# Moving two products with V and one softmax division inside a transformer block on one core

## The reference, cut to what matters

```
x = x + attn_block(layernorm(x))       # inside: attention over a window of 15 neighbours, 16 heads of 16, then an MLP 256->1024->256
z = layernorm(x)
main = gelu(z @ W1m + b1m) @ W2m + b2m # 256 -> 1024 -> 256
logits = mean(z, over the tokens) @ w_gate + b_gate      # the two best of 8 experts, weights gate_w
expert_out = sum over the two of gate_w * (gelu(z @ W1e + b1e) @ W2e + b2e)
out = x + a * main + (1 - a) * expert_out
```

## Time and profile before

| what | value |
|---|---|
| median of 3 runs | 2020.44 us (2018.67 to 2022.75) |
| profiled execution: its time, its span | 2019.08 us, 2017.4 us |
| PE busy | 1983.6 us, 98% of the span |
| DVE, ACT, POOL busy | 73%, 56%, 46% of the span |
| mean granted TensorE clock | 0.996 |

### The profile page before, as it was taken

How to read it: one execution, slowest core, us unless ns; L and a number is a source line. 1 busy time by engine, 2 the same in 40 slices (tenths; PEclk the granted TensorE clock), 3 DMA queues, 4 the chain that set the end, 5 groups by cost and what they waited for, 6 DMA issues and landing times.

```text
span 2017.4 us, 37536 instructions
## 1 busy us (share of the span) xinstructions
PE 1983.6 (98%) x13456; PEld 1817.1 (90%) x13456; DVE 1470.9 (73%) x2466; ACT 1134.0 (56%) x1797; POOL 928.3 (46%) x909
## 2 busy tenths in 40 slices
PE   7889999999999999999999999999999999999999
PEld 6789999999999999999999999999999999999998
DVE  7577786877868678686877868678686786868743
ACT  4455565655556565565555556555564655655554
POOL 5435255362543635345362552625436353453635
PEclk9999999999999999999999999999999999999999
DMA  3121121211102121121211202111021211212111
GB/s 106 48 63 43 49 57 33 74 53 53 53 22 79 48 66 51 32 65 42 74 52 44 55 30 74 53 53 53 30 70 48 69 48 38 63 38 74 43 57 54
DMA packets 188848, 108.79 MB, mean 54 GB/s; under 512 B 65436, under 2 KB 187640, under 8 KB 188664
## 3 DMA queue, kind: packets, MB, share of 16 engines
q1 hardware_dynamic: 188088, 105.62, 18.4%
q10 hardware_dynamic: 576, 0.79, 0.1%
HBM read 85.52 MB, written 8.39 MB: 47 GB/s over the span
## 4 chain that ended last, share of the span: by engine, by line
PE 92%; DVE 4%; issue 1%; ACT 1%; POOL 0%; SPq 0%; DMA 0%; ACTq 0%; POOLq 0%; DVEq 0%
PE psB L233 50%; PE psA L233 26%; PE psA L1061 6%; PE psA L1088 5%; PE psA L1073 3%; PE psA L982 2%; DVE pr L621 1%; DVE smax L617 1%; DVE acc L559 1%; DVE qm L586 0%; DVE hr_lo L543 0%; POOL wf_lo L424 0%; PE psA L1105 0%; ACT hr_hi L845 0%; PE psB L1111 0%
## 5 line engine op out<-in xcount | busy, mean ns | idle before, releaser
L543 DVE TENSOR_TENSOR hr_lo<-hf,hr_hi 128x512 fp32r<-128x512 f32 x512 | 488.5, 954 | 436.0 <-ACT hr_hi L845 435.4
L845 ACT ACTIVATE hr_hi<-hf 128x512 fp32r<-128x512 f32 x512 | 323.9, 633 | 269.7 <-PE psB L233 182.5
L435 POOL TENSOR_TENSOR wx_lo<-raw,wx_hi 128x512 fp32r<-128x512 f32 x256 | 395.9, 1546 | 21.4
L433 POOL TENSOR_SCALAR wx_hi<-raw 128x512 fp32r<-128x512 f32 x256 | 188.6, 737 | 358.0 <-PE psB L233 344.0
L841 ACT ACTIVATE hf<-psB,b1x 128x512 f32<-128x512 f32 x256 | 175.0, 684 | 201.7 <-PE psB L233 200.7
L233 PE MATMUL psB<-wx_hi,hr_hi 128*128 128x256 f32 x1024 | 287.5, 281 | 0.2
L233 PE MATMUL psB<-wx_hi,hr_lo 128*128 128x256 f32 x1024 | 286.4, 280 | 0.0
L233 PE MATMUL psB<-wx_lo,hr_hi 128*128 128x256 f32 x1024 | 285.7, 279 | 0.0
L449 POOL TENSOR_SCALAR kb<-kT 64x384 f32<-64x384 f32 x128 | 81.7, 639 | 358.9 <-ACT kT L861 351.0
L233 PE MATMUL psB<-z_hi,wx_hi 128*128 128x512 f32 x512 | 210.9, 412 | 0.0
L233 PE MATMUL psB<-z_hi,wx_lo 128*128 128x512 f32 x512 | 202.5, 396 | 0.0
(11 more groups left out here) (149 smaller groups left out, 5132.4 us busy)
## 6 DMA issues: line engine op xcount, KB each, us to landing
raw<-in_L_ffn_W1e SPq DMA_DIRECT2D x256, 128.0 KB, 2.2
raw<-in_L_ffn_W2e SPq DMA_DIRECT2D x256, 128.0 KB, 2.1
out_x<-acc SPq DMA_DIRECT2D x32, 256.0 KB, 2.2
xin<-in_L_attn_x SPq DMA_DIRECT2D x15, 512.0 KB, 3.8
vb<-vs SPq DMA_DIRECT2D x64, 96.0 KB
vb<-vs SPq DMA_DIRECT2D x64, 80.0 KB
tm<-in_L_ffn_b2e SPq DMA_DIRECT2D x32, 128.0 KB, 3.0
raw<-in_L_attn_fc_w SPq DMA_DIRECT2D x8, 256.0 KB, 3.6
```

Source lines behind the costliest of these rows:

```text
L433: g.tensor_scalar(wx[0][:, s, :], raw[:, s, :], 1.0, 0.0, ALU.mult, ALU.add).then_inc(w_hi.sem, 1)
L435: g.tensor_tensor(wx[1][:, s, :], raw[:, s, :], wx[0][:, s, :].bitcast(f32), ALU.subtract).then_inc(w_lo.sem, 1)
L543: v.tensor_tensor(hr[1][:, c % 2, :], hf[:, c % 3, :], hr[0][:, c % 2, :].bitcast(f32), ALU.subtract).then_inc(h_lo.sem, 1)
L845: a.activation(hr[0][:, c % 2, :], hf[:, c % 3, :], ACT.Copy).then_inc(h_hi.sem, 1)
```

## The change

Three moves, with no instruction added or removed. On TensorE `attend(0)` goes from slot 6 to the end of slot 5, right behind `scores(2)`, and `attend(1)` from slot 8 to the end of slot 7, right behind `scores(3)`. On VectorE the block with `gather` is put behind the block with `normalise` in every slot; only in slot 9 do both blocks have something to do, so that `normalise(2)` now stands in front of `gather` of f0 to f7.

```
@@ VectorE
                 for q in range(NQ + 2):
-                    if q >= 2 and there(ORDER[q - 2][0], t) and ORDER[q - 2][0] == "f" and ORDER[q - 2][1] % KH == KH - 1:
-                        gather(t, ORDER[q - 2][1])
                     if t < ROWS:
                         if q == 3:
                             normalise(t, 0)
...
                         elif q == 15:
                             norm2_apply(t, 1)
+                    if q >= 2 and there(ORDER[q - 2][0], t) and ORDER[q - 2][0] == "f" and ORDER[q - 2][1] % KH == KH - 1:
+                        gather(t, ORDER[q - 2][1])
                     if q < NQ and there(ORDER[q][0], t):
                         h_low(t, *ORDER[q], q)
@@ TensorE
                     elif q == 5:
                         scores(t, 2)
+                        attend(t, 0)
                     elif q == 6:
-                        attend(t, 0)
                         turn(t, 1)
                     elif q == 7:
                         scores(t, 3)
-                    elif q == 8:
                         attend(t, 1)
```

## The result

The changed kernel takes 2078.53 us (median of 4 runs, 2077.54 to 2080.74), against 2019.89 before in the same session. The ratio is 1.0291, with a 95% interval of 1.0275 to 1.0306: slower by 58.6 us. The prediction was 2074, with a range of 2048 to 2094.

The account below looks back on a forecast made before the run. The prediction took PE to bound the kernel. To the profiled 2019.1 us it added 42 for the chain of delays and 12 for clock falls, 2073; the median runs 1.4 above, so 2074, range 2048 to 2094.

Parts of the forecast that it names:

- What bounds the kernel: PE, in flight for 98% of the span: any new wait of PE is paid in full in each of 15 turns.
- `attend(0)`: Behind scores(2): PE waits for qm of unit 3, V's layout is covered, and turn(1) starts 0.16 us later.
- `attend(1)`: Behind scores(3): it waits for DVE to end attended(0), and PE idles some 0.6 us.
- The queue behind it: Behind attend(1): chunk_down(6), hr_hi(8), attended(1), normalise(2) and gather come later; PE idles 2.4 us at chunk_down(8).
- The sum: Over turns 1 to 15: 12 turns lose 2.9 us and 3 lose 2.4, 42 us in all.
- The clock: Behind PE's new idle time the granted clock falls in half the turns, at 1.7 us each: 12 us.
- Rival 1: The chain of delays holds in every turn but the clock does not fall: 2062.5 us; chance 0.20.
- rival 2: Clock falls every turn, or for twice as long in some: 2088 us, up to 2112; chance 0.09.
- rivals 4 and 5: 4: gather ends before PE reaches chunk_down(8), 2013.5 us, chance 0.05. 5: gains and waits cancel, 2020, chance 0.04.
- Rival 3: Shorter chain: h_low(6)'s stretch by POOL's addition resolves sooner and hr_hi(8) is earlier; 1.8 us a turn, 2047; chance 0.12.

Follow-up runs that it names:

- the run with `attend(1)` between the halves: The changed kernel with attend(1) in slot 8, between chunk_up(8) and chunk_down(6): 2078.29 us, ratio 1.0282 to the kernel before.
- two kernels related to it: The changed kernel with attend(1) between chunk_up(8) and chunk_down(6), 2078.29 us; the changed kernel with POOL's addition (line 455) four slots later, 2079.40 us.

## Why the prediction was right

**What bounds the kernel.** Right. PE without waits was the bound, and each new wait was paid in each of 15 turns.

**`attend(0)`.** V's layout was no matter: no wait for a DMA stands in front of it. That it waits for line 872 is not shown. Its idle time is 0.15 (0.30 in turn 3), and the profile puts it down to issue, that is, to nothing that it shows; in turn 9 line 872 had ended 0.25 before. In size the step was 0.2 too small: it starts 2.17 behind `scores(2)`, predicted 1.96, and `scores(3)` at 10.48, predicted 10.30. What I did not see is that this lateness passes on through `attended(1)`, 0.33 us a turn when the move is made alone. In the full change most of it is hidden behind the larger delay: where `attend(1)` waits for `attended(0)`, it starts at 12.65 with the move and at 12.64 without it (in the run with `attend(1)` alone).

**`attend(1)`.** Right in mechanism: it waits for `attended(0)`. In 7 of the 15 turns it starts at 12.65 as predicted (12.63), in the others at 12.25 (once 12.39) without a wait; I had expected 12 and 3. The wait costs 0.4 by the starts (12.65 against 12.25) and is 0.24 by the profile, where 0.6 was predicted: `scores(3)` in front of it comes 0.2 later than I had worked out.

**The queue behind it.** Right, link by link. Predicted for turn 9, as distances from `scores(2)`, and measured: `hr_hi(8)` 17.55 and 17.60; `attended(1)` done 20.95 and 20.91; the first half of `gather` 23.88 and `chunk_down(8)` at 23.86; idle time 2.4 predicted, 2.33 by the starts (`chunk_up(10)` is over at 1170.59) and 2.17 by the profile. `turn(2)` at 25.38 was predicted and is 25.34 where the clock stays up. The run with `attend(1)` between the halves shows that the link is `chunk_down(6)` and the buffers of `hr`.

**The sum.** 2.9 and 2.4 a turn, 42 us. Measured with the clock held up by filler: 37 us by the medians, 40 by the traces. The dearer turns cost 2.8 (125.0 from `turn(0)` to `turn(0)`, in turns 5 and 12 of the changed kernel and with filler), the cheaper ones 2.65 (124.85 with filler), and there were 8 cheaper ones in the changed kernel and not 3. They are less cheap than 2.4 against an ordinary turn of before: DVE is earlier there only against `scores(2)`, which was itself late. The swap alone was put at 0.7 a turn and costs 0.6; the `attend` moves at 2.2 and cost 1.9.

**The clock.** Right that it is a term of its own; too small in size. I took half of the turns at 1.7, 12 us. It falls in 13 of 15, at 1.5 us each, 20 us. This term was 8 us too small and the chain's was 2 to 5 too large, so that 2074 came nearer to 2078.5 than its parts: that much is luck.

Half of the turns was a guess between two rows of turn 0, and the one that spoke for no fall does not hold in the changed kernel. There the idle time of 2.60 us in the same place is followed by a fall. Its rows, and behind them the same stretch of the kernel before:

```profile
52.61 1.08 PE L1073 MATMUL psA<-ident,pr 128*96 128x128 f32 x8 [2.60 <-DVE pr L621]
52.00:58.00 6.00, 5.39 (x31) 5.09 (x32) 4.49 (x6) 1.08 (x2) 3.22 (x2) 0.72 0.45 132
...
52.00:58.00 6.00, 5.12 (x38) 4.72 (x39) 5.83 (x9) 1.96 (x4) 3.23 (x2) 1.00 0.44 132
```

So the length of an idle time does not by itself decide whether the clock falls, neither in turn 0 nor in turns 5 and 12. The moment plays a part, as the order in the result above suggests; what sets it stays open.

**The rivals.** Rival 1 (no fall) is out by the 13 falls and by the run with filler, rival 2 (a fall in every turn) by turns 5 and 12, and rivals 4 and 5 by the new wait in all 15 turns. Rival 3, a shorter chain, is what moving POOL's addition tried: it is worth 0.2 us a turn by the traces, not 1.1.

## What to carry to other kernels

Work moved forward on an engine that runs its list in order moves everything behind it back. Before moving it, name what is next in the list, who waits for that and through which buffer; here it was a buffer of the MLP, far from the attention step that was moved. Where the busiest engine gets a new idle time of 2 us, look at the granted clock too: the fall behind it cost 1.5 us a turn on top of the 2.65 to 2.8 of the delay. Test moves together as well as apart: here the parts made 39 us and the whole 58.6, because only the whole left an idle time behind which the clock fell. And compare like turns: two kinds of turn in one loop can make a move look worth half a microsecond that it is not.

## What the runs showed of the hardware

In the changed kernel the same idle time of 2.17 us is followed by 3.4 us at the lower clock in 13 turns and not in 2. In two kernels related to it, with 2.2 us of idle time in the same place, the clock fell in 15 and 14 turns. Idle times of 1.1 us at `turn(2)`, in the two kernels with `attend(1)` moved and no swap, were followed by no fall in 30 turns. An idle time of 2.60 us in turn 0 was followed by a fall in the changed kernel and by none before.

Useless matmuls in the idle time kept the clock up in all 15 turns and made the kernel 20 us faster. The Trainium skill (TensorE: Matmul & The Clock Gate, What's actually happening) calls the throttled state the default and says that activity releases it. The trace agrees as far as the filler goes; why the clock stayed up in turns 5 and 12 without it, no run here shows.

A VectorE instruction with two SBUF inputs (`h_low(6)`, 128x512) took 2.89 us beside POOL's addition and 0.69 when that was moved away.
